# All eight row tiles of the softmax weights transposed by 32x32 blocks and transfers, split in four bands, with a new plan of projection pieces

## The reference

```python
xn = _layernorm(x, axis=-1)
q = (x @ Wq + bq).reshape(b, h, t, dh)                       # h = 16 heads, dh = 128, t = 1024
k = (x @ Wk + bk).reshape(b, t, h, dh).transpose(0, 2, 3, 1)
v = (x @ Wv + bv).reshape(b, t, h, dh).transpose(0, 2, 1, 3)
logits = jnp.einsum('bhtd,bhds->bhts', q, k) * scale
weights = jax.nn.softmax(logits + mask, axis=-1)             # causal mask
out = jnp.einsum('bhts,bhsd->bhtd', weights, v)
out = out.transpose(0, 2, 1, 3).reshape(b, t, h * dh) @ Wo + bo
x = x + out + (silu(xn @ w_gate.T) * (xn @ w_up.T)) @ w_down.T
```

## Time and profile before

| | |
|---|---|
| median of 2 runs | 2091.11 us (2090.55 to 2091.66) |
| the profiled execution | 2090.48 us, of which the span from first to last instruction is 2088.7 us |
| PE busy | 1958.1 us, 94% of the span |
| PEld busy | 1725.2 us, 83% |
| DVE, ACT, POOL busy | 1188.4, 1222.7, 1264.1 us (57%, 59%, 61%) |
| mean granted TensorE clock | 0.985 |
| transfers | 286.56 MB, mean 137 GB/s |
| chain that ended last | PE 53%, POOL 24%, DVE 8%, issue 7%, DMA 4%, SP's queue 3%, ACT 1% |

### The profile page before, as it was taken

The page is one execution under the profiler, slowest core; times in us unless marked ns, Lnnn a source line. Parts: engine busy times, 40 slices in busy tenths (PEclk is TensorE's granted clock), DMA queues, the critical chain, the costliest instruction groups (busy, mean ns, idle before and its releaser), DMA issues.

```text
span 2088.7 us, 33761 instructions
## 1 busy us (share of the span) xinstructions
PE 1958.1 (94%) x11505; PEld 1725.2 (83%) x11505; DVE 1188.4 (57%) x2784; ACT 1222.7 (59%) x2282; POOL 1264.1 (61%) x1088
## 2 busy tenths in 40 slices
PE   7999999998899999899999989999999899999996
PEld 5888877887788888788888878888888788888885
DVE  7211111213666776576667766666777576677763
ACT  4323223224667776566667766667777576677762
POOL 4232245551666777577667765766777576677763
PEclk9999999999999999999999999999999999999998
DMA  6333365545445444455544454645444455444442
GB/s 224 98 105 111 111 202 192 177 156 177 128 128 144 120 116 129 145 152 145 139 124 117 126 149 123 173 131 141 117 117 131 143 159 147 135 118 117 137 108 79
DMA packets 182073, 286.56 MB, mean 137 GB/s; under 512 B 22496, under 2 KB 112784, under 8 KB 180624
## 3 DMA queue, kind: packets, MB, share of 16 engines
q1 hardware_dynamic: 181904, 284.41, 46.5%
HBM read 112.35 MB, written 62.91 MB: 84 GB/s over the span
## 4 chain that ended last, share of the span: by engine, by line
PE 53%; POOL 24%; DVE 8%; issue 7%; DMA 4%; SPq 3%; ACT 1%; POOLq 0%; DVEq 0%; ACTq 0%
PE s_ps L1000 17%; POOL pT_lo L692 17%; PE o_ps L1170 15%; PE t_ps L1000 10%; PE m_ps L1000 7%; POOL stage L686 6%; PE t_ps L1181 3%; SPq L576 3%; PE o_ps L1000 2%; DVE stage L976 2%; DVE pT_lo L981 1%; DMA q_dram<-raw_w 1%; DVE s_ps L964 1%; DMA xnT_lo<-xnT_dram 1%; POOL prob L686 1%
## 5 line engine op out<-in xcount | busy, mean ns | idle before, releaser
L964 DVE CUSTOM_DVE_ANT_0 s_ps<-s_ps,mask 128x128 f32<-128x128 f32 (+7 forms) x512 | 390.2, 762 | 481.3 <-PE s_ps L1000 481.2
L692 POOL TENSOR_TENSOR pT_lo<-turned,pT_hi 128x640 fp32r<-128x640 f32 (+3 forms) x256 | 508.6, 1987 | 12.0 <-ACT pT_hi L808 12.0
L686 POOL TENSOR_SCALAR stage<-stage,inv_sum 128x640 f32<-128x640 f32 (+3 forms) x256 | 246.1, 961 | 271.2 <-DVE inv_sum L972 271.1
L800 ACT ACTIVATE stage<-s_ps,neg_max 128x640 f32<-128x640 f32 (+3 forms) x256 | 244.5, 955 | 136.3 <-DVE neg_max L964 135.6
L1170 PE MATMUL o_ps<-pT_hi,v_hi 128*128 128x512 f32 (+3 forms) x768 | 270.2, 352 | 42.8 <-POOL pT_lo L692 42.8
L1000 PE MATMUL s_ps<-k_hi,q_hi 128*128 128x384 f32 (+5 forms) x768 | 281.4, 366 | 6.9 <-ACT stage L800 3.6
L808 ACT ACTIVATE pT_hi<-turned 128x640 fp32r<-128x640 f32 (+3 forms) x256 | 228.8, 895 | 73.1 <-DMA turned<-stage 72.9
L1170 PE MATMUL o_ps<-pT_hi,v_lo 128*128 128x512 f32 (+3 forms) x768 | 268.2, 349 | 0.0
L1170 PE MATMUL o_ps<-pT_lo,v_hi 128*128 128x512 f32 (+3 forms) x768 | 267.7, 349 | 0.0
L686 POOL TENSOR_SCALAR prob<-prob,inv_sum 128x128 f32<-128x128 f32 (+3 forms) x256 | 137.6, 537 | 211.7 <-DVE inv_sum L972 211.7
L976 DVE STREAM_TRANSPOSE stage<-stage 128x640 f32<-128x640 f32 (+3 forms) x256 | 262.4, 1025 | 2.0 <-POOL stage L686 2.0
(11 more groups left out here) (140 smaller groups left out, 4790.4 us busy)
## 6 DMA issues: line engine op xcount, KB each, us to landing
turned<-stage SPq DMA_DIRECT2D x1024, 104.0 KB, 2.6
q_dram<-raw_w SPq DMA_DIRECT2D x64, 512.0 KB, 3.2
q_raw<-q_dram SPq DMA_DIRECT2D x64, 512.0 KB, 4.3
wk_both<-wk_dram SPq DMA_DIRECT2D x64, 256.0 KB, 3.5
wv_both<-wv_dram SPq DMA_DIRECT2D x32, 512.0 KB, 3.3
wo_both<-wo_dram SPq DMA_DIRECT2D x32, 512.0 KB, 3.2
x_sb<-in_L_attn_x SPq DMA_DIRECT2D x8, 512.0 KB, 9.4
xnT_dram<-xnT_a_hi SPq DMA_DIRECT2D x8, 512.0 KB, 3.1
```

What stands on the lines that cost most here:

```text
L686: eng.tensor_scalar(weights(j), weights(j), inv_sum[:, j % 4:j % 4 + 1], 1.0, ALU.mult, ALU.mult).then_inc(s_norm, 1)
L692: eng.tensor_tensor(packed_tile(1, i), turned_tile(n, i), packed_tile(0, i).bitcast(F32), ALU.subtract).then_inc(s_plo, 1)
L800: eng.activation(weights(j), s_ps[j % 2][:, c0:c1].rearrange("p (k b t) -> p k b t", b=NB, t=32), ACT.Exp, bias=neg_max[:, j % 4:j % 4 + 1 ...
L964: eng.tensor_tensor_reduce(out=row, in0=row, in1=mask[:, T - L:T], scale=-1.0, scalar=BIG, op0=ALU.add, op1=ALU.min, accum_out=neg_max[:, ...
```

## The change

- All eight row tiles stay in `stage` and are transposed on DVE by 32x32 blocks. The TensorE transposes, the tile `prob` and the parts taken from `t_ps` are gone. A row of a transfer grows from 832 to 1152 numbers, and there are still 16 transfers a head.
- `turned` has one buffer. It is filled and split by **bands**: band a holds queries 32a to 32a+31 of all row tiles, 1152 numbers a partition. ACT takes the high part of bands 0 to 3 in steps 12 to 15 after the head's first; POOL takes the low part of bands 0, 2 and 3 in the same steps and DVE that of band 1 in step 13 (`s_dlo`), now from SBUF, where its low parts of weights came from PSUM before.
- Weights times V stands at steps 17, 18 and 19, chunk 0 in `o_ps`, chunk 1 in `m_ps`. Its terms with the high part of the weights come first, and only those with the low part wait for the low parts. `O_AT` has its own pair for odd heads.
- K of head n is issued in steps -2 and 0 of head n itself; V in steps 4, 5, 7, 8; y in 28, 29, 31, 32. The scores of row tiles 0 and 4 wait for the half of K that they need.
- SP loads q ahead of all transfers of the head, and `load_xnT` for the next batch ahead of the transfers of the batch's last head but one.

```diff
-SPLIT_AT = {14: (4,), 15: (5,), 16: (6,), 17: (7,)}
-Q_SPLIT_AT = {-3: 0, 2: 1}
-PV_AT = ((8, 0, 0, 4), (19, 1, 0, 2), (20, 1, 2, 4), (21, 1, 4, 8))
-O_AT = (9, 22)
+BLOCKS = VT * ROW
+TO_BAND = 16 * NB
+BAND_AT = (12, 13, 14, 15)
+DVE_BAND = 1
+POOL_BANDS = [band for band in range(NB) if band != DVE_BAND]
+Q_SPLIT_AT = {-3: 0, 0: 1}
+PV_AT = ((17, 0, 0, 4), (18, 1, 0, 4), (19, 1, 4, 8))
+O_AT = ((18, 20), (18, 22))
...
-K_AT = (1, 1)
-V_AT = (-5, -2, 3, 8)
-Y_AT = (6, 7, 15, 16)
-BANK_AT = {0: (0,), 1: (1, "m"), 3: ("m",), 6: (0,), 7: (1,)}
+K_AT = (-2, 0)
+V_AT = (4, 5, 7, 8)
+Y_AT = (28, 29, 31, 32)
+BANK_AT = {0: (0, 1), 4: ("o",), 5: (0,), 6: (1,), 7: ("m",)}
+O_BANK = ("o", "m")
...
-        prob = sb("prob", [P, 3, BANK], F32)
         stage = sb("stage", [P, 2, NB, BLOCKS, 32], F32)
-        turned = sb("turned", [P, 2, NB, BLOCKS, 32], F32)
+        turned = sb("turned", [P, NB, BLOCKS, 32], F32)
...
+            def exchange(n, bands):
+                if bands[0] == 0:
+                    eng.wait_ge(s_turn, NI * (n + 1))
+                for band in bands:
+                    if n:
+                        eng.wait_ge(s_dlo if band == DVE_BAND else s_plo, low_no(n - 1, band))
+                    for keys in range(NB):
+                        eng.dma_start(turned[32 * keys:32 * (keys + 1), band],
+                                      stage[32 * band:32 * (band + 1), n % 2, keys]).then_inc(s_land[band], 16)
...
+                if r == NH - 1 and b + 1 < B:
+                    eng.wait_ge(s_fill, piece_no[("V", n // 2, 3)] + 1)
+                    eng.wait_ge(s_fill, piece_no[("K", n, 1)] + 1)
+                    load_xnT(b + 1)
...
                 if n + 1 < NHD:
                     load_q(n + 1)
                 if n:
-                    exchange(n - 1, 1)
+                    exchange(n - 1, (0, 1))
...
+                for n, band in bands_split(g):
+                    eng.wait_ge(s_land[band], TO_BAND * (n + 1))
+                    if n and band == 0:
+                        eng.wait_ge(s_pv, pv_key_tile(n - 1, NI - 1))
+                    eng.activation(packed_band(0, band), turned[:, band], ACT.Copy).then_inc(s_phi, 1)
...
                 j = g - T_LAG
-                if 0 <= j < NG and j % NI >= VT:
+                if 0 <= j < NG:
                     eng.wait_ge(s_norm, j + 1)
                     eng.transpose(weights(j), weights(j)).then_inc(s_turn, 1)
...
+                for n, band in bands_split(g):
+                    if band == DVE_BAND:
+                        eng.wait_ge(s_phi, NB * n + band + 1)
+                        eng.tensor_tensor(packed_band(1, band), turned[:, band], packed_band(0, band).bitcast(F32),
+                                          ALU.subtract).then_inc(s_dlo, 1)
...
             def scores(g):
                 n, i = divmod(g, NI)
-                if i == 0:
-                    eng.wait_ge(s_pout, piece_no[("K", n, 1)] + 1)
                 if i % VT == 0:
+                    eng.wait_ge(s_pout, piece_no[("K", n, i // VT)] + 1)
                     eng.wait_ge(s_q, 2 * n + i // VT + 1)
...
+                for kt in range(k0, k1):
+                    for s in (0, 1):
+                        add(kt, s, 0, kt == 0 and s == 0, False)
+                if k0 == 0 and kc == 0:
+                    eng.wait_ge(s_plo, low_no(n, NB - 1))
+                    eng.wait_ge(s_dlo, low_no(n, DVE_BAND))
+                for kt in range(k0, k1):
+                    ins = add(kt, 0, 1, False, kt == last)
```

More of the change, by code:

```diff
@@ L93, in o_order @@
 def o_order():
[L95 removed]
+    at = [(NI * n + off, n, kc) for n in range(NHD) for kc, off in enumerate(O_AT[n % 2])]
     return {(n, kc): j + 1 for j, (_, n, kc) in enumerate(sorted(at))}
@@ L102, in chunks_out, with bands_split, low_no @@
 def chunks_out(g):
-    out = [(at_step(g, off), kc) for kc, off in enumerate(O_AT) if at_step(g, off) is not None]
-    return sorted(out, key=lambda chunk: O_NO[chunk])
+    return [(n, kc) for n, kc in O_NO if NI * n + O_AT[n % 2][kc] == g]
 def q_halves(g):
     return [(at_step(g, off), half) for off, half in Q_SPLIT_AT.items() if at_step(g, off) is not None]
[L113 to L121, removed]
+def bands_split(g):
+    return [(at_step(g, off), band) for band, off in enumerate(BAND_AT) if at_step(g, off) is not None]
+def low_no(n, band):
+    return n + 1 if band == DVE_BAND else len(POOL_BANDS) * n + POOL_BANDS.index(band) + 1
 def packed(i):
@@ L169, in plan_pieces, with latest_in @@
     return before, at, order, bank
+def latest_in(pieces_at, bank_of, g, bank):
+    for step in range(g - 1, max(g - NI, -1), -1):
+        for piece in pieces_at[step]:
+            if bank_of[piece] == bank:
+                return piece
+    return None
 def attention_ffn_block(nc, x, Wq, bq, Wk, bk, Wv, bv, Wo, bo, w_gate, w_up, w_down, out):
@@ L178, in attention_ffn_block @@
         latest[bank_of[piece]] = piece
[L179 to L183, removed]
-    for g in range(LAST + 1):
-        for piece in pieces_at[g]:
-            transposed_before[piece_no[piece]] = done.get(bank_of[piece], 0)
-            bank_latest[bank_of[piece]] = piece_no[piece] + 1
-        n, i = divmod(g - T_LAG, NI)
-        if 0 <= n < NHD and i < VT:
-            pieces_before[n, i] = bank_latest[i % 2]
-            done[i % 2] = VT * n + i + 1
+    chunk_before_piece, piece_before_chunk, held = {}, {}, {}
+    for g in range(LAST + 1):
+        for n, part in pv_parts(g):
+            _, kc, k0, _ = PV_AT[part]
+            if k0 == 0:
+                piece_before_chunk[n, kc] = latest_in(pieces_at, bank_of, g, O_BANK[kc])
+                held[O_BANK[kc]] = (n, kc)
+        for piece in pieces_at[g]:
+            chunk_before_piece[piece] = held.get(bank_of[piece])
     hi_no = {piece: j for j, piece in enumerate(piece for piece in pieces if piece[0] in "KV")}
@@ L308, in attention_ffn_block @@
         s_qload = sem("s_qload")
-        s_land = [sem("s_land0"), sem("s_land1")]
+        s_land = [sem(f"s_land{band}") for band in range(NB)]
         s_xload = [sem("s_xload_hi"), sem("s_xload_lo")]
@@ L400, in weights, with packed_band @@
             n, i = divmod(g, NI)
[L401 to L416 removed]
+            return stage[:, n % 2, :, packed(i), :].rearrange("p b k t -> p k b t")
+        def packed_band(part, band):
+            return pT[part][:, :, band, :]
         def q_half(part, half):
```

156 lines of the change are left out of this document (47 added, 109 removed).

## The result

| | before | after |
|---|---|---|
| median of 2 runs | 2091.11 us | 2161.45 us (2154.43, 2168.48) |
| ratio | | 1.0336, interval 1.0191 to 1.0481 |
| profiled execution, span | 2090.48, 2088.7 us | 2168.48, 2166.4 us |
| PE, DVE busy | 1958.1, 1188.4 us | 1927.4, 1290.7 us |
| ACT, POOL busy | 1222.7, 1264.1 us | 1198.0, 1339.1 us |

The change made the kernel slower, by 70 us. The forecast was 2110 us, and its own terms gave 2065 to 2130; the time lies above that and inside the outer range of 2015 to 2185. These are two runs of the changed kernel, 14 us apart, and the interval starts just under 2%. The changed kernel run again beside the first experiments took 2200.34 us, 1.0514 (1.0469 to 1.0559) of the kernel before, which took 2095.53 there: clearly slower, and above even the outer range.

A forecast was written before the change was run, and what follows sets the result against it. PE was taken as the bound. To the profiled span of 2088.7 us came 62 x (0.37 + 0.5) = +54, -24.6, -6 and -3, together +20, plus 1.8 outside it: forecast 2110 us, range 2015 to 2185.

The forecast's parts named there:

- PE's own work: PE in each head: ten transposes gone, with changes of work 1.5 us saved, leaving 21.65 us a head.
- The new wait: PE before the next head's first scores, for K's low part on VectorE: mean 2.5 us, within bounds of 1.5 to 4.
- Rival 2: VectorE reaches K in time, so PE's saving shows: wait 1.2 us, head 22.85 us, 1993 us; chance 0.18.
- The shared port: Band 1 on VectorE costs GpSimd 1.3 us; VectorE waits 0.1 us for the end of band 0's subtraction.
- rival 3: VectorE is held behind a GpSimd subtraction in band 1, 1.3 us in the mean: 25.55 us a head, 2160 us; chance 0.1.
- The clock: PE's clock falls after the wait for K in about three heads of ten: 0.5 us a head.
- I cost it at nothing since ScalarE is ahead: Band 0's transfers, issued behind the load of q, should land within 1 us of ScalarE's step 12: no cost.
- the sign that the prediction had set for rival 4: In the profile after, a wait on `turned` at ScalarE of more than 1 us.
- rival 4: Longer transfers and q's load push band 0 by 2 us or more: +1 us a head, 2172 us; chance 0.09.
- For which I give back 1 us each: Earlier `load_xnT` removes three stalls of 9.2 us but delays a head's transfers, 1 us each: -24.6 us.
- Start and end: Four pieces fewer before the first scores, -6 us; bands split as they land at the end, -3 us net.

## Why the prediction missed by 51 us

- **PE's own work** (21.65 us a head): nearly right. Clean heads of the changed kernel are 23.81 - 2.10 = 21.71 and 24.47 - 0.94 - 1.57 = 21.96. The mean over all ordinary heads, 21.99 at full clock, is 0.34 above the term; with the loads moved it is 21.80, so about half of the excess goes with the late bands. Why is not known.
- **The new wait** (2.2 us at the end of an even head; 0.8 and 2.0 in an odd one): right in place and cause, and nearly in size, 2.10, and 0.94 with 1.57. VectorE's list from 1019.82 to the end of `k_lo` at 1028.64 takes 8.82 us, the prediction's sum without the first 0.2 is 8.9. K one step earlier shows that this list is the cause: it gives 101 us back.
- **Rival 2** (VectorE is in time) fell: it would have been 1993. Its reason, idle time of VectorE over a quarter of the loop, was there and didn't help, since the list in front of K had none: after, VectorE is busy without a gap from 1019.82 to 1028.6.
- **The shared port.** In the profile after, VectorE's band 1 takes 1521 ns in the mean of 51 (600 to 1900 us), against 1.35 + 0.1 forecast. Beside GpSimd instructions it ran from 1.31 to 1.94 us. Where GpSimd is at a subtraction or a normalisation as it starts, its time follows a sum fitted to these rows, 1.21 us plus what that has left:

```profile
1074.10 1.88 DVE L961 TENSOR_TENSOR pT_lo<-turned,pT_hi 128x1152 fp32r<-128x1152 f32 x1
```

```profile
1073.97 0.81 POOL L679 TENSOR_SCALAR stage<-stage,inv_sum 128x640 f32<-128x640 f32 x1
...
1075.33 2.09 POOL L670 TENSOR_TENSOR q_lo<-q_raw,q_hi 128x512 fp32r<-128x512 f32 x1 [0.55 <-ACT q_hi L733]
```

GpSimd ends at 1074.78, 0.68 us after VectorE's start, and 0.68 + 1.21 = 1.89. (The 1.21 is only a fit: the shortest band 1 took 1.31 us, and the one with no GpSimd instruction beside it 1.36.) The other way, a GpSimd instruction that starts within band 1 is stretched:

```profile
1021.39 1.52 DVE L961 TENSOR_TENSOR pT_lo<-turned,pT_hi 128x1152 fp32r<-128x1152 f32 x1
```

```profile
1021.67 1.91 POOL L679 TENSOR_SCALAR stage<-stage,inv_sum 128x640 f32<-128x640 f32 x1
```

GpSimd's normalisation of 640 columns, started 0.28 us into band 1, takes 1.91 us (799 ns in the kernel before). From 600 to 1925 us the sum holds within 0.1 us in 44 of 52 cases. In the other eight GpSimd's normalisation stands 0.09 to 0.10 us ahead in the trace and is yet the one that was stretched, to 2.0 us, while band 1 took 1.32. So rival 3's mechanism is real, and only its price was wrong: about 0.2 us in the mean above the shortest times of 1.31, where it asked for 1.3 us more. That its time, 2160 us, is close to the first measured one is chance. The Trainium skill (SBUF — State Buffer, "SBUF: two separate sides") says that whichever engine starts first keeps the port pair for its whole instruction; the traces agree in the 44 cases, both ways, and leave the others open, where the two starts lie within 0.1 us.

- **The clock** (0.5 us a head): right, 0.50. It fell 19 times in heads 4 to 61, three of these inside the long waits at the changes of batch; the other 16 in 58 heads are the three of ten that were forecast. Fourteen of them came behind the wait at the end of an even head (1.97 to 4.12 us, 29 such waits), two behind the pair at the end of an odd head.
- **"I cost it at nothing since ScalarE is ahead"**, of band 0, is the step that failed. ScalarE waited 96 times at `turned`, for 150 us, 1.56 us in the mean, which is the sign that the prediction had set for rival 4, and this reached PE 31 times in 58 heads. I had the load of q in the account but not those of K's, V's and the output's weights, which start just ahead of the transfers as well, and I counted the time of the issue, not of the landing. Rival 4 had this mechanism (2 us late, +1 us a head); it measured 0.31 a head directly. Taking it out gave more, 87 us on top of K early: against K early in the same session, waits for exponentials fell from 80.3 to 9.9 us and half clock from 27.3 to 3.4 us, while the waits for `pT_lo` and `oT_odd_lo` rose by 15; 9 of the 87 us lie outside heads 4 to 61.
- **"For which I give back 1 us each"**, the `load_xnT` ahead of transfers, failed as well: in one such head ScalarE waited 7.74 us and PE 4.66. The three took 30.9, 32.4 and 31.3 us, 6.3 more than an ordinary head in the mean; before they took 9.3 more. So about two thirds of the stall stayed, now at the bands.
- **Start and end** were -6 and -3; measured -4.0 and +0.7. At the end PE waits 10.95 us for band 0's high part, where before it waited 8.84 for GpSimd's low part.

The two terms about landing, costed at almost nothing, hold 34 of the 48 us; PE's own work holds 19, and the waits on VectorE came out 8 below the forecast. That the first time lies within the stated range owes something to luck: with the same mechanisms the rerun, at 2200 us, lies outside it.

**Open.** Why the changed kernel took 2161 us in one session and 2200 in another: the same terms grew, but what decides how often a band is late was not tried. Nor was why an odd head with K early and the loads moved is 0.8 us longer than its two waits explain, what band 1 on VectorE adds to K's lateness by itself, or the place of `load_xnT` by itself.

## What to carry to other kernels

Taking work off the busiest engine pays only if what is moved elsewhere still reaches it in time: write out the list of the engine that serves it, item by item, in the steps before each hand-over, and put the last operand one step earlier if the list is longer. Cost a transfer from its issue to its landing with every load that starts in the few us ahead of it on the same DMA engines, and give such loads a second buffer so that they can go when the engines are idle. Try remedies together before giving one up: here each alone gave a tie with the kernel before (1.0007 and 1.0066), and both together 0.9593. The changed kernel stood at 1.0336 or 1.0514; against the second the two gains simply add, so the ties did not mean that a remedy was worth nothing.

## What the runs showed of the hardware

- A subtraction of two SBUF tensors on VectorE and GpSimd's subtraction or normalisation wait for each other: band 1 took 1.31 to 1.94 us, in 44 of 52 cases what GpSimd had left plus 1.21 us, and a normalisation of 799 ns on GpSimd became 1.9 us.
- 16 transfers of 144 KB a head, with three loads ahead of them, fill the DMA engines to a share of 0.95 at about 220 to 265 GB/s; one transfer landed after 5.71 us, the median is 3.8 us. It is 3.2 us with the loads elsewhere, and 104 KB ones took 2.7 us.
- Waits of 1.97 to 2.10 us in front of the scores, with none of the others close by, were enough to bring the clock down to 0.50 in some heads (behind 2.02 us at 1028.70) and not in others; a wait of 1.57 us did so only twice, 3.2 us behind one of 1.20 or 1.39 us. 6 matmuls in the wait cut the time at half clock from 109.2 to 27.3 us and gave 31 us.
